# Reordering the vector engine's bias additions and transposes in a fused attention and mixture-of-experts kernel

## The chip, the cores and the metric

The kernel runs on one core of one Trainium2 chip. The metric is the device time of one execution in microseconds. TensorE is called PE here, VectorE DVE, ScalarE ACT, GpSimd POOL and SyncE SP, as in the profile.

## The reference

```python
xn = layernorm(x)                                  # x: 2 x 4096 x 512, float32
qkv = xn(windows of 64 rows) @ qkv_w + qkv_b       # 16 heads of 32
attn = softmax(q @ k.T * scale + rel_pos_bias)     # in each window
a = (attn @ v) @ proj_w + proj_b
scores = (xn @ Wg.T).T                             # 8 experts
top_vals, token_idx = top_k(scores, 8192 / 8)      # each expert takes 1024 rows
h = silu(xg @ W1.T) * (xg @ W3.T);  y = (h @ W2.T) * softmax(top_vals)
out = x + a + scatter_add(y)
```

## The kernel before

The program has two blocks, one behind the other: `attention_block` (up to about 898 us of the profile) and `expert_block`, which the change leaves alone. Each engine has its own instruction list, written out by hand in order, and semaphores join them. Nothing is scheduled at run time: an instruction that waits holds up all that stands behind it on its engine.

**Chunks, groups and segments.** The 8192 rows are worked in 16 chunks of 512. A chunk has four groups of four heads; group s = 4c + m is group m of chunk c. A float32 product is made of three passes over a high and a low part (`split3`, L59 to L61), so one 512-column output of 512 inputs takes 12 matmuls. For each group PE makes q and k (`project_q`, `project_k`), the scores (`scores`, L860, 64 small matmuls) and probabilities times v (`pv`, L923). The segments of a chunk are the stretches between two `scores`; the third segment is the one behind `scores(s+1)`. In it PE makes q and k of group s+2, then three of the four tiles of the output projection of the chunk before (`project_out(c-1, 0)` to `(c-1, 2)`), then `pv(s, 0)` and `scores(s+2)`; then come `project_out(c-1, 3)`, q and k of group s+3, `pv(s+1, 1)` and `scores(s+3)`.

**The way of one group.** PE's scores lie in PSUM banks 0 to 3. DVE's `add_bias` (L1219, and the row maximum L1224) moves them to SBUF and frees the banks; POOL subtracts the maximum (`subtract_max`, L517); ACT takes the exponential (`exponentials`, L651); DVE sums (`normaliser`, L1228 and L1232); POOL multiplies (`normalise`, L533); DVE transposes 32-blocks (`turn_probs`, L1271); ACT copies (`own_blocks`, L647); SP's DMAs spread the blocks (`spread_probs`, L370); then PE can do `pv`. ACT's `q_part` (L631) and `k_part` (L656) take q and k from PSUM banks 6 and 7, which `project_out` uses again: `project_out(c-1, 0)` waits for the last low part of the chunk before (`o_lo_part(s-1, 3)`, L1289) and for `q_part(s+2)`, and `project_out(c-1, 1)` for `k_part(s+2)`. `project_out(c-1, 2)` and the next q and k wait for `finish_rows(c-1, t)` (L1237), with which DVE adds a tile to the residual and frees its bank.

**The next chunk.** Its normalised rows come back from DRAM in 32-blocks. DVE's `turn_blocks` (four transposes, L1196) turns them, ACT's `xt_hi_part` (L625) makes the high part, POOL's `xt_lo_part` (L542, four tiles) the low part. `turn_blocks_ahead` (L1201) turns a chunk that is ten further on, for the gate, in chunks 2 to 7.

**Searching.** Chunks 9 to 14 have `hunt_chunk` on ACT and DVE. In chunks 9 to 13 the eight experts' thresholds are searched in 16 rounds of two bits. A round is: `prepare` on DVE (thresholds L1330, two comparisons L1335, one more L1336 that counts by itself), `count_hits` on ACT (L669) for the first two, a small product on PE over partitions (`hunt(c, n)`, L948), then `take` (L1315) and `keep` (L1322, L1323) on DVE, and the next `prepare`. The product writes into bank 3, one of the scores' banks: `hunt(c, n)` waits for the `add_bias` of the group before it, `hunt(c, 5)` for that of group s+2. Chunk 13 also chooses among ties (L1366 to L1382), chunk 14 writes the experts' lists (L1348, L127 to L147).

**POOL's list.** In a searching chunk it is: subtract and normalise of s-1, two residual tiles, subtract and normalise of s, two residual tiles, subtract and normalise of s+1, then two tiles of `xt_lo_part(n)`, then subtract and normalise of s+2, then the other two tiles. In chunks 1 to 8 all four tiles stand ahead of the subtraction of s+2.

**First pass.** Chunk 0 has an order of its own. Its `first_xt(1)` makes chunk 1's transposes on PE into banks 0 to 3, ACT and DVE take the high and low parts from there (`first_xt_hi`, L620; `first_xt_lo`, L1206), and `first_gate(1)` (L829) makes its gate scores. `split_hi` and `split_lo` (L605, L1161) are units of the weights' high and low parts.

Of the kernel before, what the change touches and what calls it, by code (L numbers as in the profile page):

```python
# [205 lines left out]
def attention_block(nc, d, lists):  # L206
# [3 lines left out]
    with ctx:  # L210
# [54 lines left out]
        G_BANKS, G_BANK, GF_BANK = (OT2, KB), 2, 3  # L265
# [219 lines left out]
        def _(pool):  # L485
# [51 lines left out]
            def xt_lo_part(c, tiles=range(KC)):  # L537
                if c < FAR:
                    pool.wait_ge(gate_mm, c + 1)
                for k in tiles:  # L540
# [16 lines left out]
            def chunk(c):  # L557
# [16 lines left out]
                if n < NCH:  # L574
                    xt_lo_part(n, (0, 1) if c >= HUNT else range(KC))
# [6 lines left out]
                if HUNT <= c < NCH - 1:  # L582
                    xt_lo_part(n, (2, 3))
# [18 lines left out]
        def _(act):  # L602
# [91 lines left out]
            def hunt_chunk(c):  # L694
# [22 lines left out]
                q_part(s + 2, 2)  # L717
                exponentials(s + 1)
                k_part(s + 2, 2)
# [64 lines left out]
            split_hi(6)  # L784
            split_hi(7)
            own_blocks(0)
            q_part(2, 2)
            exponentials(1)
            k_part(2, 2)
            first_xt_hi(1)  # L790
# [21 lines left out]
        def _(pe):  # L812
# [9 lines left out]
            def first_gate(c):  # L822
# [3 lines left out]
                for k in range(0, KC, 2):  # L826
                    for j in range(4):
                        x_part = (xt_hi, xt_lo)[j % 2][c][:, k + j // 2, :].bitcast(F32)
                        i = nc.tensor.matmul(ps[32 * j:32 * (j + 1), G_BANKS[c], :], wg[:, k + j // 2, :], x_part,  # L829
# [172 lines left out]
            def first_chunk():  # L1002
# [15 lines left out]
                project_k(1, 1)  # L1018
                project_v(0, 2)
                project_v(0, 3)  # L1020
                scores(1)
# [3 lines left out]
                project_q(2, 2)  # L1025
                pe.wait_ge(v_ready, 4)
                project_k(2, 2)
                pe.wait_ge(s_ready, 2)
                first_xt(1)
                pe.wait_ge(gate_sb_ready, 1)  # L1030
                pv(0, 0)
                pe.wait_ge(xt_ready, 2 * KC)
                scores(2)

                pe.wait_ge(k_ready, 3)
                first_gate(1)
                pe.wait_ge(raw_lo, Q_SPLIT[3])
                project_q(3, 3)
                pe.wait_ge(gate_sb_ready, 2)
# [117 lines left out]
        def _(dve):  # L1157
# [50 lines left out]
            def gate_rows(c):  # L1208
                dve.wait_ge(gate_mm, c + 1)
                if c >= 1:  # L1210
                    dve.wait_ge(gate_stored, 64 * c)
                nc.vector.tensor_copy(g_sb[:, :], ps[:, G_BANK if c >= 2 else G_BANKS[c], :]).then_inc(gate_sb_ready, 1)
# [201 lines left out]
            def hunt_chunk(c):  # L1414
# [44 lines left out]
                o_lo_part(s - 1, 3)  # L1459
                if listing:  # L1460
                    then(v.tensor_scalar(part_i, pos_i, 7, None, ALU.logical_shift_right))
                    then(to_experts(lists.slot_a, part_i))
                turn_blocks(c + 1, *range(KC))

                add_bias(s + 1, 1)
                prepare(c, 4)
                normaliser(s + 1)
                finish_rows(c - 1, 0)
# [29 lines left out]
            def chunk(c):  # L1498
# [20 lines left out]
                turn_blocks(n, *range(KC))  # L1519

                add_bias(s + 1, 1)
                o_lo_part(s - 1, 3)
                if FAR < j <= NCH:
                    turn_blocks_ahead(j - 1, *range(KC))
                normaliser(s + 1)
# [494 lines left out]
```

## Time and profile before

| | us |
|---|---|
| three runs | 1975.03, 1978.11, 1980.72 |
| median | 1978.11 |
| the profiled execution, its own time | 1978.15 |
| its span | 1976.4 |
| granted clock over the span | 0.997 |
| PE busy | 1939.4 (98%), 16755 matmuls |
| DVE, ACT, POOL busy | 1161.4, 648.4, 595.2 |

The profiled execution took 1.75 us more than the span of its instructions; that part lies outside the kernel's work. Busy time of PE is an overlap of pipelined matmuls: each is shown longer than the distance from one start to the next. Times of an instruction are its start in us from the start of the span, and then its length. Idle time in brackets is that of the engine just ahead of the instruction, with what ended it.

### The profile page before, as it was taken

Reading aid. Unit: us, or ns where it says so; the run is one execution under the profiler, and the core shown is the slowest. Engines: PE = TensorE matmul, PEld = TensorE weight load, DVE = VectorE, ACT = ScalarE, POOL = GpSimd, SP = SyncE. Lnnn points to the kernel's source line nnn. Section 1 sums busy time; section 2 is a strip of 40 time slices with the busy share of each in tenths; the row PEclk is TensorE's granted clock in tenths of the full one; section 3 lists DMA queues with packets and bytes.
Section 4 is the critical chain, followed back from the end, with each engine's and each line's share of the span. In section 5 each row is a group of like instructions: output and inputs, shape, how many; then the busy total and the mean of one; then the engine's idle time right before and its main releaser. Section 6 shows DMA issues by size and latency. Waiting matters only on the chain.

```text
span 1976.4 us, 39583 instructions
## 1 busy us (share of the span) xinstructions
PE 1939.4 (98%) x16755; PEld 1571.7 (80%) x16755; DVE 1161.4 (59%) x1661; ACT 648.4 (33%) x953; POOL 595.2 (30%) x410
## 2 busy tenths in 40 slices
PE   8999999999999999999999999999999999999998
PEld 7777777777778887778788888888888888888886
DVE  7787887876888877776444345443543453434321
ACT  4333333333344343323333332332332323323321
POOL 2445445445354444541211220212112202121111
PEclk9999999999999999999999999999999999999999
DMA  7466565663323332234433442532433435324311
GB/s 203 131 174 188 169 175 155 174 158 121 87 81 87 87 87 82 66 109 158 97 118 86 88 114 76 132 84 60 129 85 83 104 89 127 82 60 135 64 22 22
DMA packets 172720, 214.65 MB, mean 109 GB/s; under 512 B 31776, under 2 KB 105888, under 8 KB 172576
## 3 DMA queue, kind: packets, MB, share of 16 engines
q1 hardware_dynamic: 146096, 154.92, 27.8%
q0 software_dynamic: 14336, 33.56, 9.6%
q10 hardware_dynamic: 12144, 24.12, 3.4%
q8 instruction: 107, 1.75, 0.4%
q14 instruction: 37, 0.30, 0.1%
HBM read 128.13 MB, written 51.38 MB: 91 GB/s over the span
## 4 chain that ended last, share of the span: by engine, by line
PE 51%; DVE 1%; SPq 1%; ACT 0%; issue 0%; DMA 0%; POOL 0%; POOLq 0%
PE ps_e L59 17%; PE ps_e L60 17%; PE ps_e L61 17%; SPq L199 1%; PE ps_e L159 1%; DMA raw<-in_w 0%; ACT w_hi L1775 0%; DVE xn L1896 0%; DVE w_lo L1890 0%; DVE hm L1922 0%; DVE xgt_lo L1901 0%; DVE x_f L147 0%; DVE hot_more L147 0%; DVE hot_v L137 0%; POOL out_rows L1739 0%
## 5 line engine op out<-in xcount | busy, mean ns | idle before, releaser
L59 PE MATMUL ps_e<-xgt_hi,w_hi 128*128 128x512 f32 x1024 | 401.4, 392 | 0.0
L60 PE MATMUL ps_e<-xgt_lo,w_hi 128*128 128x512 f32 x1024 | 398.8, 389 | 0.0
L61 PE MATMUL ps_e<-xgt_hi,w_lo 128*128 128x512 f32 x1024 | 398.7, 389 | 0.0
L1922 DVE TENSOR_TENSOR hm<-ps_e,silu 128x512 f32<-128x512 f32 x128 | 88.4, 691 | 456.4 <-PE ps_e L61 455.7
L1739 POOL DMA_INDIRECT out_rows<-x_res,idx x64 | 100.6, 1572 | 429.7 <-ACT x_res L1807 415.9
L61 PEld LDWEIGHTS ps_e<-xgt_hi,w_lo 128*128 128x128 f32 x1024 | 192.3, 188 | 40.0
L59 PEld LDWEIGHTS ps_e<-xgt_hi,w_hi 128*128 128x128 f32 x1024 | 192.3, 188 | 39.1 <-DVE xgt_lo L1901 0.2
L60 PEld LDWEIGHTS ps_e<-xgt_lo,w_hi 128*128 128x128 f32 x1024 | 192.4, 188 | 38.7
L188 POOL DMA_INDIRECT x_in<-xn_rows,idx x64 | 77.7, 1213 | 476.6 <-DVE idx L180 304.0
L59 PE MATMUL ps<-xt_hi,wqk_hi 128*128 128x512 f32 x512 | 206.2, 403 | 2.7 <-POOL xt_lo L542 1.5
L1795 ACT ACTIVATE h_hi<-hm 128x512 fp32r<-128x512 f32 x128 | 80.9, 632 | 383.9 <-DVE hm L1922 383.9
L59 PE MATMUL ps_e<-w_hi,h_hi 128*128 128x512 f32 x512 | 200.0, 391 | 1.9 <-DVE got L167 1.9
L61 PE MATMUL ps<-xt_hi,wqk_lo 128*128 128x512 f32 x512 | 200.2, 391 | 0.0
L60 PE MATMUL ps_e<-w_lo,h_hi 128*128 128x512 f32 x512 | 200.1, 391 | 0.0
L61 PE MATMUL ps_e<-w_hi,h_lo 128*128 128x512 f32 x512 | 200.1, 391 | 0.0
L60 PE MATMUL ps<-xt_lo,wqk_hi 128*128 128x512 f32 x512 | 199.8, 390 | 0.0
L517 POOL TENSOR_TENSOR s_sb<-s_sb,s_max 128x1024 f32<-128x1024 f32 x64 | 122.8, 1920 | 249.5 <-DVE s_max L1224 244.6
L533 POOL TENSOR_TENSOR pn_sb<-p_sb,s_rec 128x1024 f32<-128x1024 f32 x62 | 119.3, 1924 | 161.5 <-DVE s_rec L1232 139.8
L1908 DVE TENSOR_TENSOR h_lo<-hm,h_hi 128x512 fp32r<-128x512 f32 x128 | 88.7, 693 | 94.1 <-ACT h_hi L1795 94.1
L647 ACT ACTIVATE pt<-pn_sb 128x1024 f32<-128x1024 f32 x62 | 65.8, 1061 | 183.9 <-DVE pn_sb L1271 183.8
L1807 ACT ACTIVATE x_res<-ps_e,weight 128x512 f32<-128x512 f32 x64 | 43.1, 689 | 252.6 <-PE ps_e L61 252.6
L59 PEld LDWEIGHTS ps<-xt_hi,wqk_hi 128*128 128x128 f32 x512 | 96.1, 188 | 27.7 <-POOL xt_lo L542 3.3
(199 smaller groups left out, 3400.9 us busy)
## 6 DMA issues: line engine op xcount, KB each, us to landing
x_f<-in_w SPq DMA_DIRECT2D x48, 512.0 KB, 3.9
raw<-in_w SPq DMA_DIRECT2D x48, 512.0 KB, 3.7
x_res<-in_x SPq DMA_DIRECT2D x16, 1024.0 KB, 5.7
xn<-x_in SPq DMA_DIRECT2D x256, 64.0 KB, 2.0
pt<-pn_sb SPq DMA_DIRECT2D x248, 64.0 KB
out_rows<-x_res ACTq DMA_DIRECT2D x15, 1024.0 KB, 4.2
xn_rows<-xt_plain SPq DMA_DIRECT2D x8, 1024.0 KB, 4.4
x_in<-xn_rows SPq DMA_DIRECT2D x28, 256.0 KB, 4.5
```

What stands on the lines that cost most here:

```text
L59: nc.tensor.matmul(out, w_hi, x_hi, start=start, stop=False)
L60: nc.tensor.matmul(out, w_hi, x_lo, start=False, stop=False)
L61: return nc.tensor.matmul(out, w_lo, x_hi, start=False, stop=stop)
L188: nc.gpsimd.indirect_dma_start(out=k.x_in[:, t, :], out_offset=None, in_=xn_rows, in_offset=bass.IndirectOffsetOnAxis(ap=k.idx[par][:, til ...
L517: nc.gpsimd.tensor_tensor(s_sb[:, :, :, :], s_sb[:, :, :, :], s_max[:, :].rearrange("p (t h) -> p t h", t=TT).unsqueeze(3) .to_broadcast([ ...
L533: nc.gpsimd.tensor_tensor(halves_first(pn_sb[:, :]), p_sb[:, :, :, :].rearrange("p t h (j c) -> p (t h) j c", c=QD), s_rec[:, :].unsqueeze ...
L647: nc.scalar.activation(pt[s % 2][:, :, :, :, :].rearrange("p i t h q -> p (i t h q)"), pn_sb[:, :], ACT.Copy).then_inc(pt_own, 1)
L1739: nc.gpsimd.indirect_dma_start(out=d["out"], out_offset=bass.IndirectOffsetOnAxis(ap=lists.idx[par][:, tile0 + t:tile0 + t + 1], axis=0), ...
L1795: nc.scalar.activation(h_hi[:, m, :], hm[:, m % 2, :], ACT.Copy).then_inc(h_hi_ready, 1)
L1807: nc.scalar.activation(y[:, t, :], ps[:, DOWN + t, :], ACT.Copy, scale=weight[par][:, s:s + 1]).then_inc(y_ready, 1)
L1908: v.tensor_tensor(h_lo[:, m, :], hm[:, m % 2, :], h_hi[:, m, :].bitcast(F32), ALU.subtract).then_inc(h_ready, 1)
L1922: v.tensor_tensor(hm[:, m % 2, :], ps[:, 2 * (m % 2) + 1, :], silu[:, m % 2, :], ALU.mult).then_inc(hm_ready, 1)
```

## The change

- DVE, chunks 1 to 8 (`chunk`): `turn_blocks(n)` moves from ahead of `add_bias(s+1, 1)` and `o_lo_part(s-1, 3)` to behind them; `turn_blocks_ahead` moves behind `normaliser(s+1)`. Chunk 15 has a list of its own on DVE, which stays.
- DVE, chunks 9 to 14 (`hunt_chunk`): `add_bias(s+1, 1)` and `turn_blocks(c+1)` stand right behind `o_lo_part(s-1, 3)` in this order, ahead of the lists' work; `finish_rows(c-1, 0)` moves ahead of `normaliser(s+1)`.
- ACT, chunks 9 to 14: `k_part(s+2, 2)` moves ahead of `exponentials(s+1)`.
- POOL, chunks 9 to 14: all four tiles of `xt_lo_part(n)` stand ahead of the subtraction of s+2.
- First pass: `first_xt(1)` moves from behind `project_k(2, 2)` to ahead of `project_v(0, 2)`, `first_gate(1)` from behind `scores(2)` to ahead of `project_k(2, 2)`, its bank from KB to OT2; ACT and DVE take the parts sooner, and the last two units of weights later.

```diff
-        G_BANKS, G_BANK, GF_BANK = (OT2, KB), 2, 3
+        G_BANK, GF_BANK = 2, 3
...
@@ POOL, chunk
...
                 if n < NCH:
-                    xt_lo_part(n, (0, 1) if c >= HUNT else range(KC))
+                    xt_lo_part(n)
...
                 normalise(s + 2)
-                if HUNT <= c < NCH - 1:
-                    xt_lo_part(n, (2, 3))
...
@@ ACT, hunt_chunk
                 q_part(s + 2, 2)
+                k_part(s + 2, 2)
                 exponentials(s + 1)
-                k_part(s + 2, 2)
...
@@ ACT, first pass
             k_part(1, 1)
-            split_hi(6)
-            split_hi(7)
+            first_xt_hi(1)
             own_blocks(0)
             q_part(2, 2)
+            split_hi(6)
             exponentials(1)
             k_part(2, 2)
-            first_xt_hi(1)
+            split_hi(7)
             own_blocks(1)
...
@@ PE, first_chunk
                 project_k(1, 1)
+                pe.wait_ge(s_ready, 1)
+                first_xt(1)
                 project_v(0, 2)
                 project_v(0, 3)
+                pe.wait_ge(xt_ready, 2 * KC)
                 scores(1)
...
                 project_q(2, 2)
+                pe.wait_ge(gate_sb_ready, 1)
+                first_gate(1)
                 pe.wait_ge(v_ready, 4)
                 project_k(2, 2)
-                pe.wait_ge(s_ready, 2)
-                first_xt(1)
-                pe.wait_ge(gate_sb_ready, 1)
+                pe.wait_ge(gate_sb_ready, 2)
                 pv(0, 0)
-                pe.wait_ge(xt_ready, 2 * KC)
                 scores(2)
-                pe.wait_ge(k_ready, 3)
-                first_gate(1)
                 pe.wait_ge(raw_lo, Q_SPLIT[3])
                 project_q(3, 3)
-                pe.wait_ge(gate_sb_ready, 2)
                 project_k(3, 3)
...
@@ DVE, hunt_chunk
                 v_part(c, 3)
                 o_lo_part(s - 1, 3)
+                add_bias(s + 1, 1)
+                turn_blocks(c + 1, *range(KC))
                 if listing:
                     then(v.tensor_scalar(part_i, pos_i, 7, None, ALU.logical_shift_right))
                     then(to_experts(lists.slot_a, part_i))
-                turn_blocks(c + 1, *range(KC))
-                add_bias(s + 1, 1)
                 prepare(c, 4)
+                finish_rows(c - 1, 0)
                 normaliser(s + 1)
-                finish_rows(c - 1, 0)
                 turn_probs(s + 1)
...
@@ DVE, chunk
                 v_part(c, 3)
-                turn_blocks(n, *range(KC))
                 add_bias(s + 1, 1)
                 o_lo_part(s - 1, 3)
+                turn_blocks(n, *range(KC))
+                normaliser(s + 1)
                 if FAR < j <= NCH:
                     turn_blocks_ahead(j - 1, *range(KC))
-                normaliser(s + 1)
...
@@ DVE, first pass
             v_part(0, 2)
+            first_xt_lo(1)
             turn_probs(0)
             v_part(0, 3)
             add_bias(1, 1)
+            gate_rows(1)
             split_lo(6)
-            split_lo(7)
             normaliser(1)
-            first_xt_lo(1)
             turn_probs(1)
             add_bias(2, 2)
-            gate_rows(1)
             o_lo_part(0, 0)
+            split_lo(7)
             normaliser(2)
```

## Rows read from the trace of the kernel before

**Rows 1.** The page's busy times of the whole span, by engine.

```profile
PE 1939.4 (98%) x16755; PEld 1571.7 (80%) x16755; DVE 1161.4 (59%) x1661; ACT 648.4 (33%) x953; POOL 595.2 (30%) x410
```

**Rows 2.** Waits of PE, whole span: us in total, times, longest us.

```profile
PE ps L59 <- ACT k_sb L656: 7.8, 11, 2.4
PE ps L59 <- DVE ot_lo L1289: 3.5, 5, 1.1
PE ps L860 <- DVE xt_lo L1206: 2.2, 1, 2.2
...
PE ps L59 <- POOL xt_lo L542: 1.5, 4, 0.5
```

**Rows 3.** Timeline of chunk 4's third segment: DVE, then PE.

```profile
249.84 2.49 DVE L1196 STREAM_TRANSPOSE xt_plain<-xn 128x512 f32<-128x512 f32 x4 [0.62 <-DMA xn<-xn_rows]
...
255.34 0.50 PE L59 MATMUL ps<-wp_hi,ot_hi 128*128 128x512 f32 x1 [0.56 <-DVE ot_lo L1289]
```

**Rows 4.** Timeline of PE in the third segments of chunks 11 and 14.

```profile
638.40 0.39 PE L60 MATMUL ps<-wp_lo,ot_hi 128*128 128x512 f32 x1
638.62 0.39 PE L61 MATMUL ps<-wp_hi,ot_lo 128*128 128x512 f32 x1
639.60 0.50 PE L59 MATMUL ps<-wp_hi,ot_hi 128*128 128x512 f32 x1 [0.59 <-ACT k_sb L656]
...
803.41 0.50 PE L59 MATMUL ps<-wp_hi,ot_hi 128*128 128x512 f32 x1 [2.21 <-ACT k_sb L656]
```

**Rows 5.** Timeline of DVE, then POOL, in chunk 11's third segment.

```profile
639.15 1.21 DVE L1228 TENSOR_REDUCE s_sum<-p_sb 128x16 f32<-128x1024 f32 x1
...
640.56 0.63 DVE L1237 TENSOR_TENSOR x_res<-ps,x_res 128x512 f32<-128x512 f32 x1
...
644.79 0.38 DVE L1323 SCALAR_TENSOR_TENSOR key<-kept_i,key 128x1 int32<-128x1 int32 x1
645.20 0.16 DVE L1330 SCALAR_TENSOR_TENSOR thr<-pattern,key 128x3 int32<-128x3 int32 x1
645.40 0.88 DVE L1335 TENSOR_SCALAR x_f<-x_f,thr 128x512 bf16<-128x512 f32 x2
...
646.86 0.69 DVE L1237 TENSOR_TENSOR x_res<-ps,x_res 128x512 f32<-128x512 f32 x1
647.46 1.22 DVE L1219 TENSOR_TENSOR s_sb<-ps,rel 128x1024 f32<-128x1024 f32 x1
...
640.72 1.91 POOL L533 TENSOR_TENSOR pn_sb<-p_sb,s_rec 128x1024 f32<-128x1024 f32 x1 [2.84 <-DVE s_rec L1232]
642.59 2.56 POOL L542 TENSOR_TENSOR xt_lo<-xt_plain,xt_hi 128x512 fp32r<-128x512 f32 x2
```

**Rows 6.** Counting products of PE in chunks 9, 11 and 12.

```profile
543.35 0.28 PE L948 MATMUL ps<-cnt,same 128*128 128x3 f32 x2
...
650.02 0.28 PE L948 MATMUL ps<-cnt,same 128*128 128x3 f32 x2
...
665.99 0.28 PE L948 MATMUL ps<-cnt,same 128*128 128x3 f32 x2
```

**Rows 7.** ACT's last count ahead of the product of 665.99.

```profile
665.18 0.19 ACT L669 ACTIVATION_READ_ACCUMULATOR x_f<-x_f 128x1 f32 x1
```

**Rows 8.** POOL's four tiles in one run, chunk 4.

```profile
261.25 5.04 POOL L542 TENSOR_TENSOR xt_lo<-xt_plain,xt_hi 128x512 fp32r<-128x512 f32 x4
```

**Rows 9.** The scan that ranks ties, DVE, chunk 13.

```profile
750.59 1.44 DVE L1366 TENSOR_TENSOR_SCAN xt_f<-hot_v,xt_f 128x512 f32<-128x512 f32 x1
```

**Rows 10.** Timeline of the first pass: DVE, ACT, then PE.

```profile
38.92 1.23 DVE L1219 TENSOR_TENSOR s_sb<-ps,rel 128x1024 f32<-128x1024 f32 x1
...
57.79 0.69 ACT L656 ACTIVATE k_sb<-ps,qk_bias 128x512 f32<-128x512 f32 x1 [1.36 <-PE ps L61]
...
58.58 0.90 PE L860 MATMUL ps<-k_sb,q_sb 32*64 32x64 f32 x64
```

**Rows 11.** Busy times of chunks 10 to 12: PE, PEld, DVE, ACT, POOL.

```profile
563.20:722.92 159.72, 157.44 (x2144) 127.81 (x2139) 133.32 (x220) 70.89 (x122) 76.23 (x49) 1.00 0.29 81
```

More of the change, by code:

```diff
@@ L535, in normalise, with xt_lo_part @@
                                             ALU.mult).then_inc(norm_ready, 1)
-            def xt_lo_part(c, tiles=range(KC)):
+            def xt_lo_part(c):
                 if c < FAR:
                     pool.wait_ge(gate_mm, c + 1)
-                for k in tiles:
+                for k in range(KC):
                     pool.wait_ge(xt_hi_ready, KC * c + k + 1)
@@ L828, in first_gate @@
                         x_part = (xt_hi, xt_lo)[j % 2][c][:, k + j // 2, :].bitcast(F32)
-                        i = nc.tensor.matmul(ps[32 * j:32 * (j + 1), G_BANKS[c], :], wg[:, k + j // 2, :], x_part,
+                        i = nc.tensor.matmul(ps[32 * j:32 * (j + 1), OT2, :], wg[:, k + j // 2, :], x_part,
                                              start=(k == 0), stop=(k == KC - 2))
@@ L1211, in gate_rows @@
                     dve.wait_ge(gate_stored, 64 * c)
-                nc.vector.tensor_copy(g_sb[:, :], ps[:, G_BANK if c >= 2 else G_BANKS[c], :]).then_inc(gate_sb_ready, 1)
+                nc.vector.tensor_copy(g_sb[:, :], ps[:, G_BANK if c >= 2 else OT2, :]).then_inc(gate_sb_ready, 1)
             def add_bias(s, m):
```

## The prediction

> **What bounds the kernel now.** I read the page's busy times first: PE is busy for 1939.4 of 1976.4 us [rows 1]. No other engine comes near, so a reordering can only give back PE's waits, or add some. The list of PE's waits, read next, shows those that this change aims at: 7.8 us for the copy of K, 3.5 us for the low part of the attention output, 2.2 us for the low parts of chunk 1's rows, 1.5 us for POOL's low parts [rows 2]. Some 15 us is thus all that there is to win in place. Then I read the timeline around single waits. A wait costs more than its idle time: starts are 0.23 us apart while a matmul is shown 0.39 us long, and the first one behind a wait takes 0.50, which is 0.11 more [rows 4]. So each costs 0.27 us on top, except ahead of scores. Last, chunks 10 to 12: DVE is busy for 133.3 of 159.7 us there [rows 11]. It is second to PE by little, and what PE needs often passes through its list in order.
>
> **Part 1, chunks 1 to 8.** In chunk 4 DVE turns the next chunk's blocks for 2.49 us, 0.62 of idle time before them spent waiting for their load, and only then adds the bias and takes the low part; PE's output projection starts at 255.34 after 0.56 us of idle time [rows 3]. With the turning behind them, bias and low part come about 2.5 us sooner, and the longest of the five waits is 1.1 [rows 2]: all go. The turning itself is then needed by the gate product, one 2.7 us tile later than the projection's start, and its 2.5 us end before; the turning ahead moves 1.5 us later behind the normaliser, and its consumer stands two tiles further on; SP's load into that buffer, queued behind it, has 5 us of cover. Gain: 3.5 + 5 x 0.27 = 4.9 us. Bounds: 4.0 to 5.0.
>
> **Part 2, the first pass.** The wait of 2.2 us ahead of scores(2) [rows 2] goes, since the transposes stand 12 us sooner. But DVE now takes the four parts (2.4 us, each like the finish of 0.63 [rows 5]) ahead of its transposes of probabilities and of add_bias(1), and scores(1) needs them out of its banks. By my reckoning the part ends 0.5 us after PE could start scores(1): a new wait. add_bias(1) starts at about 42.0 instead of 38.92 [rows 10], 3 us later; the maximum, POOL, the exponential and the normaliser follow by some 2.2 us, since one unit of weights has left their way. So the exponential of group 2, ahead of K's copy on ACT, is also 2 us late. Before, that copy waited for PE, and ran at 57.79, scores(3) at 58.58 [rows 10]. Now it starts at about 58.3 and scores(3) at 59.05: 0.5 us later than before, the won 2.2 spent. The lag of 2 us on DVE meets chunk 1's second v product too, which waits for K's copy with about 1 us of slack: another 0.5. Sum: +1.0. Bounds: -2.2 (nothing late) and +3 (the whole lag of add_bias(1) reaches PE).
>
> **Part 3, the searching chunks.** Take chunk 11. The projection's first tile has its last start at 638.62 [rows 4] and ends at 639.0. With K copied ahead of the exponential, the second tile follows at once: 0.59 + 0.27 = 0.86 us won. From there the changed lists run so. DVE finishes the tile (0.63, to 639.7), and only then sums and inverts (1.21 + 0.2, to 641.2); POOL normalises (1.91, to 643.1) [rows 5]. Then come four tiles of low parts: 5.04 us [rows 8], to 648.2, where there were two, 2.56 [rows 5]. Beside them DVE has its transposes and second tile, which POOL does not hold, and reaches keep and prepare at about 645.2. **These it holds.** The key took 0.38 us and ended at 645.17, just behind POOL's tile (642.59 + 2.56 = 645.15), where the threshold beside no POOL work took 0.16; then the comparisons (0.88) ran free and the finish started at 646.86 [rows 5]. With POOL in its tiles up to 648.2, key, threshold and first comparison each wait for a tile's end; whether DVE slips in between two tiles or waits for all, the comparisons start at about 648.3. Finish at 649.8, add_bias at 650.4 (before 647.46), its banks free at 651.6. PE's counting product hunt(c, 5) writes into one of these banks and waits. PE itself would be there 0.86 us before 650.02 [rows 6], at 649.15. So it waits 2.45 us and is at 651.6: **1.6 us later than before**, behind it q and k of group s+3.
> DVE is then 2.9 us late and K's copy, the exponential and ACT's counts with it, less 0.2. In the next first segment the last count ended at 665.37 [rows 7] and PE's product came at 665.99 [rows 6], 0.6 of slack; 2.7 - 1.6 - 0.6 gives 0.5 more. From there DVE's lag fits into the second segment's slack, and the third starts from PE's tile again, so it doesn't grow: 2.1 us a chunk, 6.3 for chunks 10 to 12. Bounds a chunk: -0.86 (comparisons not held; bias at 648.9, no wait) and +3.
> Chunk 9 has the long wait, 2.4 [rows 2], and wins 2.6, but its counting product then waits for the same chain: tile end 530.6, finish and normaliser to 533.0, POOL to 535.0, four tiles to 540.1, comparisons, finish and bias to 543.4, against 543.35 before [rows 6]. Net +0.1, and the late DVE costs 0.8 in the two next segments: +0.9.
> Chunk 13 has no round at that place, but the scan, which was held as well (1.44 us [rows 9]), and the choice of ties behind it meet POOL's tiles: bias 2.4 us later, PE 1.35 later at its product although 0.86 was won, and with chunk 14's first product, which waits for the next bias, +1.5. The choice's last, accumulating step under POOL is in no row; held like the scan it costs one tile (1.26), free nothing; I take held, as the scan is the nearest row. Chunk 14 wins its 2.2 + 0.27 [rows 4] and, as chunk 13 does, POOL's waits at the next chunk's start (1.5 + 4 x 0.27 in all [rows 2]), but the one-hot steps meet POOL too, its bias is 1.8 late and q of the last group 0.95; what is left with chunk 15 is +0.35.
> Sum of part 3: 0.9 + 6.3 + 1.5 + 0.35 = **+9.1**.
>
> **A rule beside the rows.** Two tiles beside held vector steps lasted 2.56 us, four without them 5.04 [rows 5, 8]: the stream is stretched by 0.04 at most. The Trainium skill, "SBUF — State Buffer", section "Who interferes with whom", says that the second to issue fully blocks until the first finishes, POOL behind DVE as well. By that rule each step that gets in would lengthen the stream, 0.16 + 0.16 us in four chunks, and the sum would be 1.3 us higher. I go by the rows.
>
> **Sum.** 1978.15 (the profiled execution, at the median's 1978.11) - 4.9 + 1.0 + 9.1 = **1983.3 us**. About 0.3%, 5.9 us, is what a measurement of this kernel can tell from no change; this lies just inside.
>
> **Rivals.**
> *A, the stream holds nothing that matters: faster.* If the comparisons slip through POOL's tiles, or PE has more slack than I see, all of the waits aimed at go: 2.6 in chunk 9, 0.86 in each of 10 to 13, 2.5 in chunk 14, 2.6 for POOL's parts, 11.1 in sum. With parts 1 and 2: 1978.15 - 4.9 + 1.0 - 11.1 = 1963.1. For it: in the third segment the four tiles are all that got longer, and the comparisons of `prepare(c, 4)` run freer than before. Against it: the key's end at POOL's end [rows 5].
> *B, half of it.* The tiles hold the search, but only one step long, say 1.3 us a chunk less, and the first pass comes out even: 1983.3 - 5 - 1 = 1977.
> *C, DVE's lag feeds on: slower.* The place is the counting product of the second segment. It decides once ACT's counts come over 0.6 us later against PE than before; from there each us goes to PE, one to one. A lag of 1.3 us left there costs 0.7 in four chunks, and the first pass at its bound 2 more: 1983.3 + 2.8 + 2 = 1988. For it: DVE is busy for 83% of these chunks [rows 11]. Against: the third segment starts anew from a PE tile.
>
> **How the numbers follow.** Forecast 0.58, A 0.2, B 0.09, C 0.13. The forecast's own range is 1979 to 1988, of it 0.32 within 5.9 us of before and 0.26 above; B lies within; C above; A below. That gives faster 0.2, same 0.41, slower 0.39. The range reaches down into A and up past C: 1968 to 1990.
>
> **What would show it.** Part 1: no wait for ot_lo in chunks 2 to 7. Part 2: no wait ahead of scores(2), DVE's L1219 at about 42, a wait for k_sb ahead of scores(3). Part 3: no wait of a wp product for k_sb; four L542 in a run of 5 us in chunks 9 to 14; L1335 or L1323 long beside them; and PE's L948 of hunt(c, 5) waiting over 2 us for s_sb (L1219). Wrong if L1219 of group s+2 comes within 1 us of its place before; then A holds.

## The result, and the profile after

The changed kernel takes **1987.94 us** (median of 5 runs, 1985.59 to 1989.68). The kernel before takes 1979.52 us on the same chips (5 runs, 1975.03 to 1980.72). The ratio is 1.0040, with a 95% interval of 1.0028 to 1.0052: slower by 5.5 to 10.3 us. The forecast was 1983.3 with a range of 1968 to 1990; it lies 4.6 us too low, and the loss is beyond the 0.3% inside which I had put it.

The profiled execution took 1988.94 us. The page's busy times of the changed kernel:

```profile
span 1987.2 us, 39581 instructions
PE 1943.7 (98%) x16755; PEld 1574.4 (79%) x16755; DVE 1167.1 (59%) x1661; ACT 646.6 (33%) x953; POOL 594.5 (30%) x410
```

Against [rows 1] the number of instructions is the same on every engine and the span is 10.8 us longer, PE's busy time only 4.3. So PE waits 6.5 us more, and 4.3 us more are matmuls that took longer. Both have to be found. In the changed kernel the lines of PE, ACT and DVE have numbers lower by 2 or 3: the bias is L1216 (was L1219), the counting product L946 (was L948), the comparisons L1332.

Waits of PE in the changed kernel (us in total, times, longest us):

```profile
PE ps L946 <- DVE s_sb L1216: 11.2, 6, 2.2
PE ps L858 <- issue: 3.5, 1, 3.5
...
PE ps L59 <- DVE s_sb L1216: 2.1, 2, 1.8
...
PE ps L946 <- ACT x_f L667: 1.6, 4, 0.7
...
PE ps L59 <- ACT k_sb L654: 1.2, 5, 0.4
```

Every wait at which the change aimed is gone or small: of [rows 2] the 3.5 us for ot_lo, the 1.5 us for POOL's tiles and 6.6 of the 7.8 us for k_sb. In their place stands one large kind, 11.2 us in six waits of the counting product L946 for the bias, and one that nobody had asked for, 3.5 us of "issue" in the middle of the scores.

**The search.** Chunk 11's third segment in the changed kernel, DVE, then POOL, then PE (start, us, operation, count, idle time before in brackets):

```profile
651.16 0.35 DVE L1320 SCALAR_TENSOR_TENSOR key<-kept_i,key 128x1 int32<-128x1 int32 x1
651.54 1.20 DVE L1327 SCALAR_TENSOR_TENSOR thr<-pattern,key 128x3 int32<-128x3 int32 x1
652.78 1.87 DVE L1332 TENSOR_SCALAR x_f<-x_f,thr 128x512 bf16<-128x512 f32 x2
...
655.84 1.21 DVE L1216 TENSOR_TENSOR s_sb<-ps,rel 128x1024 f32<-128x1024 f32 x1
...
647.09 1.91 POOL L533 TENSOR_TENSOR pn_sb<-p_sb,s_rec 128x1024 f32<-128x1024 f32 x1 [5.79 <-DVE s_rec L1229]
648.96 5.02 POOL L542 TENSOR_TENSOR xt_lo<-xt_plain,xt_hi 128x512 fp32r<-128x512 f32 x4
...
657.10 0.39 PE L946 MATMUL ps<-cnt,same 128*128 128x3 f32 x2 [2.04 <-DVE s_sb L1216]
```

The four tiles end one after the other at about 650.2, 651.5, 652.7 and 654.0. The key ends at 651.51, the threshold, which took 0.16 us in [rows 5], lasts 1.20 and ends at 652.74, and the two comparisons (0.88 in [rows 5]) last 1.87, the first of them to the end of the fourth tile. Of these three kinds of step, which the tiles hold, DVE gets in **one per tile**; the short steps ahead of the key (L1312, L1319), the finish and the transposes are not held. The bias then starts 20.34 us after its segment's scores (635.50). In the kernel before it was 17.75 us (629.71 to 647.46 [rows 5]). That is 2.6 us later, and PE waits 2.04.

**The first pass.** The changed kernel, DVE, then ACT, then PE:

```profile
42.46 1.21 DVE L1216 TENSOR_TENSOR s_sb<-ps,rel 128x1024 f32<-128x1024 f32 x1
...
59.07 0.68 ACT L654 ACTIVATE k_sb<-ps,qk_bias 128x512 f32<-128x512 f32 x1
...
180.86 0.86 PE L858 MATMUL ps<-k_sb,q_sb 32*64 32x64 f32 x59
185.20 0.33 PE L858 MATMUL ps<-k_sb,q_sb 32*64 32x64 f32 x5 [3.47 <-issue]
185.46 0.70 PE L59 MATMUL ps<-xt_hi,wqk_hi 128*128 128x512 f32 x1
185.95 0.63 PE L60 MATMUL ps<-xt_lo,wqk_hi 128*128 128x512 f32 x1
...
189.44 0.39 PE L60 MATMUL ps<-xt_lo,wqk_hi 128*128 128x512 f32 x1
```

The bias of the second group came at 42.46 (38.92 before [rows 10]), K's copy at 59.07 (57.79). The wait of 2.2 us ahead of scores(2) is gone. In its place stand 0.46 us ahead of scores(1) for the low parts, 1.12 us at 58.12 for the DMA that spreads the probabilities, and 0.86 us ahead of scores(3) for ACT's copy of q. The whole execution began 0.6 us later, its first copies too; chunk 1 then starts 1.96 us later than before (73.28 against 71.32), 1.3 of it from this pass. The last five lines are the surprise, two chunks further on. PE stops after 59 of the 64 score products and stands for 3.47 us with no semaphore to wait for. Then its matmuls last 0.63 us and start some 0.43 apart, where 0.39 and 0.23 are usual. Busy times of the changed kernel by stretch (PE, PEld, DVE, ACT, POOL, granted clock, DMA share, GB/s):

```profile
180.00:185.60 5.60, 2.13 (x130) 1.76 (x130) 3.67 (x7) 1.54 (x2) 0.48 (x1) 1.00 0.85 321
185.60:189.00 3.40, 3.40 (x9) 2.66 (x10) 3.02 (x3) 0.00 (x0) 0.86 (x1) 0.50 0.74 260
...
602.00:605.40 3.40, 3.40 (x9) 2.65 (x8) 2.15 (x8) 1.06 (x1) 1.90 (x1) 0.50 0.52 201
```

Behind the gap the granted clock is at its lower level, 1.2 GHz, for 3.4 us; the same happens at 602.0, just behind the 2.02 us wait of chunk 10. Such a stretch does 9 matmuls where some 15 would fit. Gap and clock together put PE's start of the next segment back by 4.96 us.

Taking the start of each scores in the two traces gives the whole account. Chunks 1 to 8: 5.1 us won. First pass: 1.6 lost, 0.3 of it in chunk 1. Gap at 185: 5.0 lost. Chunks 9 to 15: 8.5 lost, of which some 1.1 are the low clock at 602.0. Later first copies: 0.6. Sum 10.6 of the 10.8.

### The profile page after: what moved, and what is told of

The parts are those of the page before. It is cut to its first block, busy times and chain, and to the rows that moved or that the text cites. A ratio compares the mean times of both kernels' runs of the same rounds, so it can differ in the third digit from the quotient of the medians.

```text
span 1987.2 us, 39581 instructions
## 1 busy us (share of the span) xinstructions
PE 1943.7 (98%) x16755; PEld 1574.4 (79%) x16755; DVE 1167.1 (59%) x1661; ACT 646.6 (33%) x953; POOL 594.5 (30%) x410
## 4 chain that ended last, share of the span: by engine, by line
PE 51%; DVE 1%; SPq 1%; ACT 0%; issue 0%; DMA 0%; POOL 0%; POOLq 0%
PE ps_e L59 17%; PE ps_e L61 17%; PE ps_e L60 17%; SPq L199 1%; PE ps_e L159 1%; DMA raw<-in_w 0%; ACT w_hi L1772 0%; DVE xn L1893 0%; DVE w_lo L1887 0%; DVE hm L1919 0%; DVE xgt_lo L1898 0%; DVE x_f L147 0%; DVE hot_more L147 0%; DVE hot_v L137 0%; POOL out_rows L1736 0%
## 5 line engine op out<-in xcount | busy, mean ns | idle before, releaser
L59 PE MATMUL ps_e<-xgt_hi,w_hi 128*128 128x512 f32 x1024 | 400.9, 392 | 0.0
L59 PEld LDWEIGHTS ps_e<-xgt_hi,w_hi 128*128 128x128 f32 x1024 | 192.2, 188 | 38.9 <-DVE xgt_lo L1898 0.2
L59 PE MATMUL ps<-xt_hi,wqk_hi 128*128 128x512 f32 x512 | 207.5, 405 | 3.0 <-DVE s_sb L1216 1.8
L59 PE MATMUL ps_e<-w_hi,h_hi 128*128 128x512 f32 x512 | 199.9, 390 | 2.2 <-DVE got L167 2.2
L59 PEld LDWEIGHTS ps<-xt_hi,wqk_hi 128*128 128x128 f32 x512 | 96.7, 189 | 27.8 <-issue 3.6
```

What stands on the lines that cost most here:

```text
L59: nc.tensor.matmul(out, w_hi, x_hi, start=start, stop=False)
```

## The experiments

Two theories stood against each other for the search. **T**: POOL's run of four tiles holds key, threshold and comparisons, and the chain of finish, sum and normaliser that starts this run is late. **R**: something else in the new order (the K copy ahead, the bias's new place) delays the bias. For the gap: chance, the place of the instructions in PE's program, or the order of the first pass.

All times are medians; ratios are to the kernel before, run beside them on the same chip (1981.44 us for the first four kernels, 1980.40 for the next four, 1979.10 for the last four).

| kernel | us | ratio, 95% interval |
|---|---|---|
| after again | 1988.72 | 1.0036 [1.0023, 1.0048] |
| after, POOL two and two | 1978.05 | 0.9982 [0.9973, 0.9991] |
| after, finish behind | 1978.08 | 0.9985 [0.9976, 0.9994] |
| before, part 1 alone | 1976.10 | 0.9972 [0.9960, 0.9984] |
| after, old first pass | 1982.32 | 1.0006 [0.9997, 1.0015] |
| before, four tiles alone | 1986.06 | 1.0026 [1.0015, 1.0036] |
| after, counting form | 1985.66 | 1.0027 [1.0016, 1.0038] |
| before, the three safe edits | 1966.18 | 0.9927 [0.9913, 0.9940] |
| after, 20 idle products | 1989.56 | 1.0048 [1.0032, 1.0063] |
| before, new first pass alone | 1986.83 | 1.0037 [1.0023, 1.0051] |
| safe edits, three and one | 1966.88 | 0.9938 [0.9924, 0.9951] |
| after, 8 idle products | 1988.54 | 1.0048 [1.0032, 1.0063] |

### 1. After again

No edit.

> The changed kernel again, unaltered, for one open point: in its first profile TensorE stands still for 3.47 us in the middle of the scores at 185 us (put down to issue, no semaphore) and then runs at half clock for 3.4 us, 4.96 us lost in all against the kernel before. If that is a chance event of one execution, there is no such gap of over 1 us here and the profiled execution takes 1983 to 1985 us. If it belongs to the changed order of instructions, it is at 185 us again and the execution takes 1986 to 1989 us.

The gap is there again, 2.9 us at 184.4 (waits of PE, this execution):

```profile
PE ps L946 <- DVE s_sb L1216: 9.9, 5, 2.1
PE ps L858 <- issue: 2.9, 1, 2.9
```

So it is no chance event of one execution. The expected 1986 to 1989 us came too.

### 2. Two and two

```diff
-                    xt_lo_part(n)
+                    xt_lo_part(n, (0, 1) if c >= HUNT else range(KC))
...
                 normalise(s + 2)
+                if HUNT <= c < NCH - 1:
+                    xt_lo_part(n, (2, 3))
```

> After, with POOL's four K tiles of the searching chunks split two and two again (two before the hunt, two inside it); all else as changed. Theory (the run of four tiles holds the search): the waits of the hunt's products for s_sb fall from 11.2 us in six events to 2 us or less, TensorE's waits for POOL's K tiles come back (about 1.5 us in all), and the time falls by some 8 us to 1979 to 1981. Rival (it is the finishing of the rows ahead of the normaliser that delays the chain): the waits stay at 1.5 us or more each, time 1985 to 1988.

10.7 us faster than after on the same chip, 1978.05. Waits of PE:

```profile
PE ps L59 <- POOL xt_lo L542: 4.2, 8, 1.4
...
PE ps L59 <- DVE s_sb L1218: 0.7, 1, 0.7
...
PE ps L948 <- DVE s_sb L1218: 0.6, 1, 0.6
```

And DVE's timeline of chunk 11:

```profile
645.48 0.16 DVE L1329 SCALAR_TENSOR_TENSOR thr<-pattern,key 128x3 int32<-128x3 int32 x1
645.68 0.88 DVE L1334 TENSOR_SCALAR x_f<-x_f,thr 128x512 bf16<-128x512 f32 x2
...
647.74 1.22 DVE L1218 TENSOR_TENSOR s_sb<-ps,rel 128x1024 f32<-128x1024 f32 x1
```

With two tiles ahead, threshold and comparisons run free, and the waits for the bias fall from 13.3 us (L946 and L59) to 1.3. R falls: K's copy and the bias stand as in the changed kernel. The waits for POOL's tiles come back at 4.2 us, not 1.5, which fits a chain that still starts late with the finish ahead of the normaliser. That the gain is 10.7 and not 8 lies in part behind the attention: no stretch of low clock at 963 there, and that half is 2.3 us shorter than in the repeat of after (1076.1 us against 1078.4). In the searching chunks this execution also has one stretch of low clock, the repeat three.

### 3. The finish behind

```diff
                 prepare(c, 4)
-                finish_rows(c - 1, 0)
                 normaliser(s + 1)
+                finish_rows(c - 1, 0)
```

> After, with finish_rows(c-1, 0) back behind the normaliser's sum in hunt_chunk; all else as changed, the four K tiles in one run on POOL too. POOL's chain then begins some 1.7 us sooner. Theory: the hunt's products wait 0.3 to 0.5 us each for s_sb where they waited 2.0, which gives back 6 to 8 us: 1979 to 1982. Rival (what delays the bias is the K copy ahead on ACT or the new place of the bias, not POOL's chain): waits still 1.5 us or more each, 1986 to 1988.

10.6 us faster than after, 1978.08. Waits of PE:

```profile
PE ps L946 <- DVE s_sb L1216: 3.4, 5, 1.6
```

And the timeline of chunk 11, DVE, then PE:

```profile
645.62 1.21 DVE L1327 SCALAR_TENSOR_TENSOR thr<-pattern,key 128x3 int32<-128x3 int32 x1
646.86 1.86 DVE L1332 TENSOR_SCALAR x_f<-x_f,thr 128x512 bf16<-128x512 f32 x2
...
649.91 1.21 DVE L1216 TENSOR_TENSOR s_sb<-ps,rel 128x1024 f32<-128x1024 f32 x1
...
651.17 0.39 PE L946 MATMUL ps<-cnt,same 128*128 128x3 f32 x2 [0.23 <-DVE s_sb L1216]
```

The hold is unchanged (1.21 and 1.86), it only comes earlier. Counted from the segment's scores the bias starts after 18.63 us where after has 20.34: the 1.7 us expected. Chunk 9 keeps a wait of 1.6. So **either half of the cause, taken away, brings the kernel back to the level of the kernel before**. That isn't yet all that was lost: experiment 8 has neither half, and shows what each costs by itself.

### 4. Part 1 alone

```diff
                 v_part(c, 3)
-                turn_blocks(n, *range(KC))
                 add_bias(s + 1, 1)
                 o_lo_part(s - 1, 3)
+                turn_blocks(n, *range(KC))
+                normaliser(s + 1)
                 if FAR < j <= NCH:
                     turn_blocks_ahead(j - 1, *range(KC))
-                normaliser(s + 1)
```

> The kernel before with the first part of the change alone (in chunks 1 to 8 the bias of the segment after next is added ahead of the turns). The five waits of TensorE for ot_lo (4.9 us) are gone and nothing comes in their place: 1974 to 1975 against 1979.5 for the kernel before, a ratio near 0.9975. Rival (the hold moves to the turns, and PE waits for them instead): 1979, no change.

5.5 us faster than before (3.2 to 7.9 by the interval). By the starts of the scores it wins 5.1 us from chunk 2 to chunk 8, and of the waits of PE from 100 to 460 us one kind is left:

```profile
PE ps L59 <- ACT k_sb L656: 0.3, 2, 0.2
```

In the profiled execution 1.7 us are lost again behind the 2.25 us wait at 49.4, where the kernel before lost nothing after the same wait. The 5.1 us are counted against one execution of the kernel before, with 3.5 us of waits for ot_lo. Experiments 6 and 10 have the order of before in chunks 2 to 8, and the waits there came to 1.5 and 1.8 us: from the scores of chunk 2 to those of chunk 9 they took 381.2 and 381.3 us (the gap of experiment 10 taken off), the kernel before 383.0, this one 377.9. Against them part 1 is worth 3.4 us. Busy times of this kernel from 50.60 to 54.10:

```profile
50.60:54.10 3.50, 3.50 (x18) 1.01 (x11) 2.73 (x3) 1.43 (x2) 1.21 (x1) 0.51 0.17 42
```

And of the kernel before in the same stretch:

```profile
50.60:54.10 3.50, 3.50 (x25) 2.00 (x18) 3.34 (x4) 1.39 (x2) 1.24 (x1) 1.00 0.20 50
```

The same instructions behind the same wait, 18 against 25 matmuls: at the lower and at the full clock.

### 5. The old first pass

The edit is the first pass of the diff, undone (PE, ACT, DVE and the gate's bank).

> After, with the first pass of the kernel before (the second chunk's transposes as late as they were); all else as changed. The changed first pass ends some 1.3 us later in the trace of after than in that of before, so this kernel should be 1 to 2 us faster than after, 1986 to 1987. Rival (the later end is only the later start of the loads in that execution): as after, 1988.

Far more than expected: 1982.32 us, a ratio of 1.0006 where after has 1.0040 and its repeat 1.0036, some 6 to 7 us. Against the repeat of after each scores from chunk 2 on starts 0.2 us earlier up to 181 us, and 4.6 us earlier from then on to the end of chunk 15. The scores at 180.43 run through (timeline of PE):

```profile
180.43 0.91 PE L858 MATMUL ps<-k_sb,q_sb 32*64 32x64 f32 x64
```

So the gap with its clock costs 4.4 us between these two. The rest is the pass itself: this execution lost some 1.9 us at 51.0 to a fall of the clock behind the wait that the old order keeps, and the traces are level there for that reason alone.

### 6. Four tiles alone

```diff
-                    xt_lo_part(n, (0, 1) if c >= HUNT else range(KC))
+                    xt_lo_part(n)
...
-                if HUNT <= c < NCH - 1:
-                    xt_lo_part(n, (2, 3))
```
(on the kernel before)

> The kernel before with one edit: the four K tiles of the searching chunks stand in one run on POOL ahead of the hunt. Theory: the run holds key, threshold and comparisons, and waits of 1 to 2.5 us each for s_sb appear at the hunt's product in chunks 9 to 12, against 1.5 us saved at POOL's tiles: 3 to 8 us slower than the kernel before. Rival (the tiles hold nobody): 1.5 us faster or no change.

5.1 us slower than before (3.0 to 7.1). The wait for s_sb is there (waits of PE):

```profile
PE ps L59 <- ACT k_sb L654: 8.3, 12, 2.4
PE ps L946 <- DVE s_sb L1217: 3.4, 5, 1.2
```

The time is as expected, the waits are not: they are 0.6 us each in chunks 9 to 12, where 1 to 2.5 were expected. One moved pair of tiles thus turns 1.5 us of visible waits into 5 us of loss. The bias of chunk 11 is 2.1 us later after its scores than before (19.82 us against 17.75).

### 7. The counting form

```diff
-  v.tensor_scalar(hits[:, j, :], gate_s, thr[:, j:j + 1].bitcast(F32), None, ALU.is_ge).then_inc(hits_ready, 1)
+  v.tensor_scalar(hits[:, j, :], gate_s, thr[:, j:j + 1].bitcast(F32), 0.0, ALU.is_ge, ALU.add,
+                  accum_out=spare[:, j:j + 1]).then_inc(hits_ready, 1)
```
(on after)

> After, with the first two comparisons of each search in the accumulating form, which in the trace is not held up while POOL copies tiles. Theory: of the delay of the bias, the part of the two comparisons (about 1.2 us) goes, that of key and threshold stays: waits for s_sb 0.8 to 1.0 us each where they were 2.0, and 3 to 5 us faster than after. Rival (the comparisons are not where the time is lost, the chain only starts late): no change.

The timeline of chunk 11, DVE, then PE:

```profile
652.17 1.21 DVE L1328 SCALAR_TENSOR_TENSOR thr<-pattern,key 128x3 int32<-128x3 int32 x1
653.41 0.75 DVE L1333 TENSOR_SCALAR_CACHE_REDUCE x_f<-x_f,thr 128x512 bf16<-128x512 f32 x1
...
657.28 0.38 PE L947 MATMUL ps<-cnt,same 128*128 128x3 f32 x2 [1.59 <-DVE s_sb L1217]
```

The comparisons are no longer held, as expected: POOL's fourth tile ends at 654.6, and each takes 0.67 from its start to the next one's (653.41, 654.08, 654.75). But free in the old form they take 0.44 each, so the form costs 0.46 a pair of the 1.0 that it saves, and key and threshold stay held. The wait falls by 0.45 us, from 2.04 to 1.59, not by 1.2. The time falls by 1.8 us (against the repeat) to 2.6, less than expected, and the intervals of the ratios overlap. The traces don't give even that to the edit: the attention ends 0.35 us sooner than in after, and the rest lies in the expert block, which took 1076.5 us for 1078.5 without its stretch of low clock. The shorter wait is shown, a gain in time is not.

### 8. The three safe edits

On the kernel before: part 1, and in the searching chunks

```diff
                 q_part(s + 2, 2)
+                k_part(s + 2, 2)
                 exponentials(s + 1)
-                k_part(s + 2, 2)
...
                 o_lo_part(s - 1, 3)
+                add_bias(s + 1, 1)
+                turn_blocks(c + 1, *range(KC))
                 if listing:
...
-                turn_blocks(c + 1, *range(KC))
-                add_bias(s + 1, 1)
```

POOL's tiles, the finish and the first pass as before.

> The kernel before with those parts of the change that the theory says cost nothing: the bias ahead of the turns everywhere, the K copy on ACT ahead in the searching chunks; but POOL's tiles two and two, the finishing of the rows behind the normaliser, and the old first pass. The waits for ot_lo (4.9 us) and for k_sb (some 8 us) go, those for POOL's tiles (1.5 us) stay: 1966 to 1970, a ratio of 0.993 to 0.996 to the kernel before. Rival (each wait that goes is given back at the next bank): 1975 to 1979.

1966.18 us: 14.5 us faster than the kernel before (11.9 to 17.2) and the best of all. Waits of PE:

```profile
PE ps L59 <- POOL xt_lo L542: 1.9, 4, 0.8
...
PE ps L59 <- ACT k_sb L656: 1.0, 5, 0.2
```

No wait for s_sb, none for ot_lo. Key, threshold and comparisons of chunk 11 run free, and the bias starts 16.76 us after its scores, 1.0 sooner than before. Nothing that went was given back elsewhere, and no stretch of low clock lies between the start and the last microseconds. In the traces, against the kernel before, it begins 0.6 us later, wins 4.9 in chunks 2 to 8 and 6.9 from chunk 9 on, and 1.2 in the expert block, where the kernel before has a stretch of low clock at 952.

This kernel also completes experiments 2 and 3. All four kernels in this table have the bias and K's copy where the change puts them:

| from the scores of chunk 9 to the expert block | us | stretches of low clock |
|---|---|---|
| two and two, finish behind (this one) | 383.8 | 0 |
| two and two, finish ahead (experiment 2) | 391.8 | 1 |
| four tiles, finish behind (experiment 3) | 390.3 | 0 |
| four tiles, finish ahead (after) | 399.2 | 1 |

The kernel before took 390.7. So the tiles alone cost 6.5 us and the early finish alone 8.0, its low clock included; both together cost 15.4. Experiments 2 and 3 gave back one half each, and stood level with the kernel before in these chunks only since the two good edits paid for the other half.

### 9 and 12. Where the gap sits

```diff
-            for _ in range(24):
+            for _ in range(20):
                 nc.tensor.matmul(ps[:, SP, 0:P], ident[:, :], ident[:, :], start=True, stop=True)
```
(and `range(8)` in the other)

> After, with 20 idle products on TensorE at the very start where there were 24; everything else as changed. In the four profiled kernels with the new first pass besides after, TensorE stands 2.8 to 3.5 us at 185 us inside the scores with nothing to wait for while an instruction fetch is under way, and in none of the five with the old one. This moves every later instruction of TensorE by a few places in its program and by almost nothing in time. If the gap hangs on where the instructions lie, it moves or goes and the time falls by up to 4.6 us to 1983 to 1984; if it hangs on the order and the times of the first pass, it stays at 184 to 186 us and the time stays at 1987 to 1989.

> After, with 8 idle products on TensorE at the very start where there were 24: a larger shift of every later instruction than the one with 20. If the gap at 185 us hangs on where the instructions lie, it moves or goes here (time down by up to 4.6 us, less what a colder start costs); if it hangs on the order and the times of the first pass, it is at 183 to 186 us again.

With 20, the gap ends at the same time, but begins 1.3 us later (183.07 against 181.72), behind the scores and two matmuls into the next group (timeline of PE):

```profile
181.50 0.91 PE L858 MATMUL ps<-k_sb,q_sb 32*64 32x64 f32 x64
185.44 0.58 PE L61 MATMUL ps<-xt_hi,wqk_lo 128*128 128x512 f32 x1 [2.37 <-issue]
```

Each product counts as two matmuls in the trace, so 4 products fewer make 8 matmuls fewer ahead of everything. Busy times from the start to the gap in after; the first count in brackets is that of matmuls:

```profile
0.00:185.15 185.15, 175.14 (x2243) 137.25 (x2243) 142.96 (x216) 64.87 (x87) 74.43 (x63) 1.00 0.59 169
```

And with 20 idle products:

```profile
0.00:185.40 185.40, 175.03 (x2242) 136.77 (x2243) 143.53 (x217) 64.98 (x87) 74.50 (x63) 1.00 0.60 168
```

The count is the same to within one (2243 in each of the five others that have it), while the operation is not, nor the moment at which PE stops. So the gap goes with the **number of the instruction from the start of PE's program**, as far as one shift of eight matmuls can show it. With 8 products there is none; that kernel's first scores come 2.2 us later than those of after, with a wait of 3.8 us for the first rows, and it comes out as slow. The time fell in neither. With 20 the gap only moved. With 8 its absence is worth 4.9 us against after by the starts of the scores; 2.5 had gone into the late start, and 1.8 went in chunks 7 to 15, where the clock fell twice and in after once. Whether 32 matmuls or 2.2 us drove the gap away there isn't settled.

### 10. The new first pass alone

The first pass of the diff on the kernel before.

> The kernel before with the new first pass alone. In the traces of after and of the version with the old first pass the difference is 0.24 us by the end of chunk 3's first segment and 4.6 us behind it, by the gap at 185 us and the half clock behind it. So if the gap comes with the new first pass whatever stands in the other chunks, this kernel is 4 to 5 us slower than before (ratio 1.002); the rival, that the gap needs the rest of the change too, gives no change (0 to +0.5 us) and no gap.

7.3 us slower than before (4.6 to 10.1): more than the 4 to 5 expected, and the rival is out. Waits of PE:

```profile
PE ps L860 <- issue: 2.9, 1, 2.9
```

All seven profiles with the new first pass and 24 or 20 idle products show the gap, none of the six with the old one does (the kernel before among them), whatever the other chunks are. By the starts of the scores the kernel began 0.3 us later, the pass itself put PE back by 2.0, the gap by 4.2, and a stretch of low clock at 809.5 by 1.6; chunk 15 took 0.8 more and the expert block 0.2, and in chunks 2 to 8 it had 1.7 less of waits for ot_lo and what they cost. That makes up the 7.5 us between the two spans. In the records of the DMA queue that fetches instructions, the packets with the old first pass begin at 171.5, 175.3 and 183.2 us (experiment 5) and with the new at 171.9, 182.8 and 187.5 (after): one fetch comes 7.5 us late. In all seven kernels PE goes on 2.2 to 2.4 us behind the start of that packet. The records don't say whose instructions it carries; that PE waited for it is argued from this, and no run shows it directly. Why the order of the first pass delays it stays open.

### 11. Three and one

```diff
-                    xt_lo_part(n, (0, 1) if c >= HUNT else range(KC))
+                    xt_lo_part(n, (0, 1, 2) if c >= HUNT else range(KC))
...
-                    xt_lo_part(n, (2, 3))
+                    xt_lo_part(n, (3,))
```
(on experiment 8)

> The best version with POOL's K tiles of the searching chunks split three and one. Its four waits for POOL's tiles (1.9 us in all, 0.8 us at most) mostly go; the third tile holds the search by 1.27 us more. In the version with four tiles and the early chain the waits for s_sb were 0.7 us each, so two tiles less one leave a slack of some 0.6 us: no waits for s_sb in chunks 10 to 12, perhaps 0.5 us in chunk 9. 1 to 2 us faster than with two and two: 1964 to 1966. Rival (no slack): waits for s_sb of 1.3 us each, 1968 to 1971.

Waits of PE:

```profile
PE ps L948 <- DVE s_sb L1219: 0.8, 2, 0.6
...
PE ps L59 <- DVE s_sb L1219: 0.5, 2, 0.3
```

DVE's timeline of chunk 11:

```profile
638.95 1.21 DVE L1330 SCALAR_TENSOR_TENSOR thr<-pattern,key 128x3 int32<-128x3 int32 x1
640.19 0.88 DVE L1335 TENSOR_SCALAR x_f<-x_f,thr 128x512 bf16<-128x512 f32 x2
```

1966.88, not to be told from experiment 8; the 1 to 2 us expected are not won. The waits for POOL's tiles fall from 1.9 to 0.4 us, and 1.3 us of waits for the bias have come. The hold goes tile by tile: beside two tiles threshold and comparisons are free (experiment 2), beside three the threshold is held and the comparisons are free, beside four the threshold and the first comparison are held (experiment 3).

## Why the prediction was right or wrong

**Part 1, right.** Forecast -4.9; the trace shows -5.1, experiment 4 -5.5. All five waits went and nothing came for them. That the sizes agree so closely is in part luck: two other executions of the old order had about half of these waits, and against them the gain is 3.4.

**Part 2, wrong, and the largest miss.** Forecast +1.0, bounds -2.2 to +3. What I had worked out is what the timeline shows: a wait of 0.46 us ahead of scores(1) (forecast 0.5), DVE's bias at 42.46 (42.0), scores(3) 0.6 us late after the 0.6 of the later start (0.5), the wait of 2.2 us gone, then 0.7 with a wait for K's copy at 69.53 (0.5) and 0.3 more in chunk 1: +1.6 in all. One sign was not met: ahead of scores(3) PE waited for q, not for K. The late exponential stood ahead of both copies on ACT, and PE had by then waited 1.12 us for the spread of the probabilities, which the forecast had at nothing. The step that failed is the one that was not written: that an order of instructions costs only through what they wait for. The gap at 185 us and the low clock behind it add 4.2 to 5.0 us; experiments 5 and 10 put the whole first pass at +6 to +7 and +7.3. The trace before showed no gap of "issue" of more than 0.3 us in the attention, so this term couldn't be read from it; the bound of +3 was too sure of the list of waits.

**Part 3, right in mechanism and nearly in size.** Forecast +9.1, trace +8.5; by the ratios of experiments 5 and 4 (1.0006 against 0.9972) it is 6.7, and the trace without the low clock at 602.0 has 7.4. So the term was some 2 us too large. Key, threshold and first comparison each waited for a tile's end, as reckoned. The bias came 2.6 us later for 2.9, the counting product waited 2.04 us for 2.45. Chunks 11 and 12 lost 1.95 and 1.98 for 2.1, chunk 10 3.3, of which some 1.1 since the clock fell there (the same chunk took 56.8 us here and 55.7 in experiment 12, with a wait of 1.92 us for 2.02 and no fall); chunk 9 0.35 for 0.9; chunk 13 1.1 for 1.5; chunks 14 and 15 -0.2 for +0.35. Experiment 6 shows that the four tiles alone make a loss of 5 us, and experiments 2, 3 and 8 that the tiles and the early finish have about equal parts in it. The prediction had both in its chain of times, but named the hold alone as the cause.

**The rule of the Trainium skill beside the rows.** The four tiles with DVE's held steps beside them lasted 5.02 us, and 5.04 without such steps in [rows 8]. By the Trainium skill, "SBUF — State Buffer", section "Who interferes with whom", the engine that issues first has the ports that DVE and POOL share for its whole instruction and the other blocks, so POOL behind DVE as fully as DVE behind POOL. The trace agrees for DVE and shows no time lost by POOL. The sum rightly went by the rows; the 1.3 us more that the prediction worked out by this rule are not seen.

**The rivals.** A (1963.1, the stream holds nothing that matters) is out: the waits for s_sb stand in the trace. With two tiles and the finish where they were, most of its gain is there: experiment 8 stands at 1966.2, and its searching chunks win 6.9 of the 11.1 us. B (1977) is out: the searching chunks lost what the forecast gave them. C's time (1988) is what was measured, yet not by its mechanism: in the second segment, the place that it names, the only wait is chunk 9's for ACT, 0.74 us where the kernel before had 0.77. In the first segments PE waits 0.3 us for ACT's counts (forecast 0.5), and DVE's lag doesn't feed on. The number was met by the gap. That 1987.9 still lies inside, at the edge of the forecast's own 1979 to 1988, is luck: nothing in the prediction stands for the gap.

**The sum.** The terms were -4.9, +1.0, +9.1; the trace has -5.1, +1.6 and +5.0, +8.5, and 0.6 from the start. Without the gap's 5.0 the median of 1987.9 would be at about 1983, as forecast and within 0.3% of before. This last is an estimate; no kernel with all of the change ran without the gap and without a late start. The agreement is better than the terms: 0.6 us of it come from the later start, and part 3 reaches its 8.5 only with 1.1 us of low clock.

## What to carry to other kernels

Before a stream of POOL tiles is moved or lengthened, look at what DVE runs beside it: each short held instruction costs it up to a whole tile, and a search is made of many short ones. An edit with good parts (the bias ahead of the turns, twice, and K's copy ahead) and bad ones (the four tiles, the early finish, the first pass) reads as a failure in the sum; taken apart, this one gave a kernel 14.5 us faster than before. Two bad parts that lengthen one chain can each seem to be all of it when one is taken away: compare also with a kernel that has neither. And after a reordering look for waits put down to "issue": they can lie far behind the place that was edited.

## What the runs showed of the hardware

- **DVE gets in one held step per POOL tile.** Beside three or four tiles of 1.26 us in a run, the threshold takes 1.20 or 1.21 us for 0.16 in chunk 11 of all nine profiled kernels that have such a run, and beside four the comparison in the plain form is held too; its accumulating form is not (0.67 us each beside the tiles), nor are transposes (1.25 us at 649.03 in after) and the finishing of rows (0.65 at 650.20). POOL's subtraction holds as well: in the kernel before the two comparisons at 636.00 took 2.56 us for 0.88 beside the one at 635.98, which lasted 1.90. The POOL tiles lost nothing (5.02 us for four with held steps beside them, 5.04 without).
- **TensorE's clock falls behind a wait of PE, but not each time.** In the 14 profiled executions, between 20 and 900 us, PE has 38 waits of 2.0 us or more; behind 20 of them, all seven gaps and 13 of the 31 others, the granted clock is at its lower level (1.2 GHz) for 3.41 us. The same wait in the same kernel does it in one execution and not in another (657.1 in after, 656.3 in its repeat). It also happened behind shorter waits, of 1.4 to 1.8 us, and twice behind two close ones of 1.1 and 0.9. A fall costs 1.6 us where PE has work, and less where a later wait takes part of it up (1.1 us in chunk 10, 0.2 in chunk 13 of the repeat). A wait of 2 us is thus worth more than its length.
- **PE can stand still with nothing to wait for**: 2.4 to 3.5 us in seven kernels, behind 2242 or 2243 matmuls from the start, while a packet of the instruction queue came late, some 120 us behind the edit that brought it on. In after DMA was busy for 0.85 of its share there.
